# A graph network on one core: one block in place of five ahead of the edge sort, and the zero fill asked for by two engines

## The reference, cut to what matters

```python
q_i = (x @ Wq).reshape(-1, 8, 8)[dst]
k_j = (x @ Wk).reshape(-1, 8, 8)[src]
w   = mlp(edge_attr_8) + mlp(edge_attr_16)        # silu(a @ W1 + b1) @ W2 + b2
alpha = (q_i * w * k_j).sum(-1) / sqrt(8) * edge_weight
out = segment_sum(alpha[..., None] * (x @ Wv)[src].reshape(-1, 8, 8), dst) / 32
x = layernorm(x + out)
# then three more layers over the same edges: 3 smoothing steps with a threshold,
# 5 powers of the normalised adjacency, 2 graph convolutions
```

## Time and profile before

| what | us |
|---|---|
| median of three runs | 8149.56 |
| the profiled execution | 8145.88 |
| its span, first to last instruction | 8144.0 |
| zero fill asked for (ACT's 100 requests) | 2.46 to 234.85 |
| first request of the sort | 414.76 |
| first scatter of the sort | 447.10 |
| last scatter of the sort | 2911.28 |
| PE busy over the span | 6943.6 (85%) |
| DVE / ACT / POOL busy | 5918.6 / 4418.0 / 2861.5 |

### The profile page before, as it was taken

The page is one execution under the profiler, slowest core; times in us unless marked ns, Lnnn a source line. Parts: engine busy times, 40 slices in busy tenths (PEclk is TensorE's granted clock), DMA queues, the critical chain, the costliest instruction groups (busy, mean ns, idle before and its releaser), DMA issues. The chain is left out here.

```text
span 8144.0 us, 280276 instructions
## 1 busy us (share of the span) xinstructions
PE 6943.6 (85%) x98699; PEld 5906.3 (73%) x98724; DVE 5918.6 (73%) x17405; ACT 4418.0 (54%) x13288; POOL 2861.5 (35%) x2957
## 2 busy tenths in 40 slices
PE   0289999999999989999996588788896899998887
PEld 0155555555555579999996588788896888897877
DVE  1266666666666679899896799799899666676556
ACT  0222222222222269999996587687796565665545
POOL 0068888888888855455454000000000000000000
PEclk9999999999999999999998799999998999998889
DMA  9222232222322247767665688787895666664545
GB/s 383 113 55 61 59 61 59 60 59 60 60 60 61 59 157 231 230 227 230 226 228 174 231 300 292 276 298 283 291 332 205 201 197 197 197 192 137 171 134 157
DMA packets 656410, 1425.57 MB, mean 175 GB/s; under 512 B 284336, under 2 KB 351662, under 8 KB 652737
## 3 DMA queue, kind: packets, MB, share of 16 engines
q1 hardware_dynamic: 538370, 1220.03, 46.6%
q0 software_dynamic: 101792, 92.82, 5.5%
q10 hardware_dynamic: 15700, 105.61, 3.2%
HBM read 982.95 MB, written 433.34 MB: 174 GB/s over the span
## 5 line engine op out<-in xcount | busy, mean ns | idle before, releaser
L243 POOL DMA_INDIRECT sorted_rows<-sort_rows,sort_row_at x1600 | 1975.2, 1234 | 518.0 <-issue 496.4
L1560 ACT ACTIVATE smooth_msg<-smooth_ps_a,smooth_w_rows 128x64 f32<-128x64 f32 x6000 | 1311.6, 333 | 313.3 <-PE smooth_ps_a L1646 297.1
L273 ACT ACTIVATE sort_count<-sort_ps_c 50x50 bf16<-50x50 f32 x1600 | 331.9, 207 | 1983.8 <-PE sort_ps_c L305 1348.2
L1341 ACT ACTIVATE poly_cast<-poly_mat 128x1536 bf16<-128x1536 uint8 x500 | 714.2, 1475 | 462.3 <-PE poly_ps L1362 362.8
L301 PEld LDWEIGHTS sort_ps_r<-sort_count,sort_hot_dt 50*125 50x125 bf16 x1600 | 283.3, 177 | 836.5 <-issue 639.1
L315 PE MATMUL sort_ps_m<-sort_w,sort_hidden 128*125 128x64 f32 x3200 | 879.3, 430 | 0.0
L1668 PE MATMUL smooth_ps_s<-smooth_msg,smooth_hot 128*128 128x64 bf16 x7500 | 769.1, 194 | 76.8 <-DVE smooth_last_part L1799 67.0
L294 PE MATMUL sort_ps_h<-sort_attrs,sort_w 24*128 24x500 f32 x800 | 812.6, 1117 | 2.5 <-DMA sort_attrs<-in_attr_t 2.5
L1668 PE MATMUL smooth_ps_s<-smooth_last_part,smooth_hot 128*128 128x64 bf16 x7500 | 763.6, 194 | 15.9 <-issue 15.9
L1668 PE MATMUL smooth_ps_s<-smooth_rest,smooth_hot 128*128 128x64 bf16 x7500 | 764.7, 194 | 14.3 <-issue 14.3
L1668 PEld LDWEIGHTS smooth_ps_s<-smooth_msg,smooth_hot 128*128 128x128 bf16 x7500 | 685.8, 99 | 111.9 <-DVE smooth_last_part L1799 68.9
(11 more groups left out here) (332 smaller groups left out, 16487.0 us busy)
## 6 DMA issues: line engine op xcount, KB each, us to landing
poly_mat<-counts_t SPq DMA_DIRECT2D x500, 400.0 KB
smooth_src<-src_rows SPq DMA_DIRECT2D x150, 960.0 KB, 5.0
smooth_hot<-hot_rows SPq DMA_DIRECT2D x150, 960.0 KB, 6.9
smooth_src<-src_rows SPq DMA_DIRECT2D x150, 640.0 KB, 6.0
smooth_hot<-hot_rows SPq DMA_DIRECT2D x150, 640.0 KB, 6.3
sorted_rows<-zeros ACTq DMA_DIRECT2D x100, 875.0 KB, 13.3
graph_edges<-sorted_rows SPq DMA_DIRECT2D x125, 700.0 KB
hot_rows<-graph_hot SPq DMA_DIRECT2D x125, 640.0 KB, 3.4
```

What stands on the lines that cost most here:

```text
L243: pool.indirect_dma_start(out=sorted_rows, out_offset=bass.IndirectOffsetOnAxis(row_at[u][:, j:j + 1], 0), in_=rows[u][:, j, :], in_offset ...
L1341: act.activation(cast[u][h][:, DVE_S:HR, :], mat[u][h][:, DVE_S:HR, :], ACT.Copy)\
L1560: last = act.activation(at[:, i, :], ps_a[g % 2][:, i * D:(i + 1) * D], ACT.Copy, scale=w_rows[u][:, c * CHUNK + i:c * CHUNK + i + 1])
```

## The change

The blocks `prepare`, `load_tables`, `project` (its first use alone; the convolutions still call it) and `split_qkv` become one block, `front`. SP asks for x, the weights and the two tables right behind the three column loads. PE transposes straight from x, four node blocks into one PSUM bank; DVE copies each four transposes at once (64 x 500) and each two products at once (125 x 384). ACT computes nothing in it. The scratch tiles of the edge tables lie in `q_parts` and `kv_parts`, so the split of q waits until the keys and blocks have landed, and it writes its remainders to `node_sums` (not in use yet) in place of `qkv`, so it needn't wait for the store of `qkv`. ACT asks for 72 of the 100 transfers of zeros in this block, SP for 28 in the sort, behind the loads of groups 0 and 1.

```diff
+ZERO_DMAS = 2 * NB
+ZERO_EARLY = 72
+def fill_zeros(eng, sorted_rows, zeros, zeroed, begin, end):
+    view = sorted_rows[0:N_SLOTS, :].rearrange("(k b) c -> k (b c)", b=NB // 2)
+    for b in range(begin, end):
+        eng.dma_start(view[b * CAP:(b + 1) * CAP, :], zeros[:]).then_inc(zeroed, 16)
 ...
+        under_kv = kv_parts[:].rearrange("p b i d -> p (b i d)").bitcast(F32)
+        under_q = q_parts[:].rearrange("p b i d -> p (b i d)").bitcast(F32)
+        ends = under_kv[:, 0:2 * NT].bitcast(I32).rearrange("p (e t) -> p e t", e=2)
+        node, lane, block_d, block_s = (under_kv[:, i * NT:(i + 1) * NT] for i in range(2, 6))
+        rest = node_sums[:].rearrange("p b c -> p (b c)")[:, 0:NB * D]
 ...
             @blk.scalar
             def _(act):
                 act.wait_ge(zeros_made, 1)
-                for b in range(2 * NB):
-                    act.dma_start(view[b * CAP:(b + 1) * CAP, :], zeros[:]).then_inc(zeroed, 16)
+                fill_zeros(act, sorted_rows, zeros, zeroed, 0, ZERO_EARLY)
 ...
             @blk.sync
+                sp.dma_start(x[:], ...).then_inc(tables_in, 16)     # Wq, Wk, Wv, ident, iota too
                 sp.wait_ge(cols_read, 2)
                 sp.dma_start(ends[:, 0, :], io["dst"]...).then_inc(rows_in, 16)
                 sp.dma_start(ends[:, 1, :], io["src"]...).then_inc(rows_in, 16)
+                sp.wait_ge(kept, NB // 2)
+                sp.dma_start(qkv_rows..., qkv...).then_inc(rows_out, 16)
                 sp.wait_ge(rows_ready, 1)
 ...
-                sp.wait_ge(rows_out, 32)
+                sp.wait_ge(rows_out, 48)
+            @blk.tensor
+                def products(i):
+                    b, e = groups[i]
+                    pe.wait_ge(turned_sb, i + 1)
+                    for j in range(b, e):
+                        if j % 2 == 0 and j >= 4:
+                            pe.wait_ge(kept, j // 2 - 1)
+                        last = nc.tensor.matmul(ps_o[j // 2 % 2][0:NL, (j % 2) * 256:(j % 2) * 256 + 3 * D],
+                                                xt[i % 2][:, (j - b) * NL:(j - b + 1) * NL], w_qkv[:], ...)
+                        if j % 2 == 1:
+                            last.then_inc(product, 1)
+                pe.wait_ge(tables_in, 96)
+                for i, (b, e) in enumerate(groups):
+                    if i >= 2:
+                        pe.wait_ge(turned_sb, i - 1)
+                    for j in range(b, e):
+                        last = nc.tensor.transpose(ps_t[i % 2][...], x[:, j, :], ident[0:NL, 0:NL])
+                    last.then_inc(turned, 1)
+                    if i >= 1:
+                        products(i - 1)
+                products(len(groups) - 1)
             @blk.vector
+                def keep(i):
 ...
+                def parts(to, whole):
+                    left = rest.rearrange("p (b d) -> p b d", d=whole.shape[2])
+                    link(dve.tensor_copy(to[:, :, 0, :], whole))
+                    link(dve.tensor_tensor(left, whole, to[:, :, 0, :], ALU.subtract))
+                    link(dve.tensor_copy(to[:, :, 1, :], left))
+                    link(dve.tensor_tensor(to[:, :, 2, :], left, to[:, :, 1, :], ALU.subtract))
 ...
+                dve.wait_ge(tables_in, 96)
+                for i in range(len(groups) + 1):
+                    keep(i)
                 dve.wait_ge(rows_in, 32)
 ...
+                dve.wait_ge(kept, NB // 2)
+                for h in two:
+                    at = slice(h * half, (h + 1) * half)
+                    parts(kv_parts[:, at], qkv[:, at, D:3 * D])
+                dve.wait_ge(rows_out, 48)
+                parts(q_parts, qkv[:, :, 0:D])
@@ sort_edges
                 for u in two:
                     loads(u, slice(u * G * TE, (u + 1) * G * TE))
+                fill_zeros(sp, sorted_rows, zeros, zeroed, ZERO_EARLY, ZERO_DMAS)
 ...
-                pool.wait_ge(zeroed, 32 * NB)
+                pool.wait_ge(zeroed, 16 * ZERO_DMAS)
```

More of the change, by code:

```diff
@@ L63, in prepare @@
[L63 to L68, removed]
+        two = range(2)
+        under_kv = kv_parts[:].rearrange("p b i d -> p (b i d)").bitcast(F32)
+        under_q = q_parts[:].rearrange("p b i d -> p (b i d)").bitcast(F32)
@@ L71, in prepare @@
+        groups = [(b, min(b + QUAD, NB)) for b in range(0, NB, QUAD)]
         with nc.Block() as blk:
@@ L105, in link, with places @@
                     dve.wait_ge(step, n[0])
-                def split(which, block, read):
-                    link(dve.tensor_copy(node[:], ends[:, which, :]))
+                def places(which, block, read):
+                    link(dve.tensor_copy(node, ends[:, which, :]))
                     if read:
                         dve.sem_inc(cols_read, 1)
[L112 to L115, removed]
@@ L126, in _ @@
[L126 to L133 removed]
+                    link(dve.tensor_scalar(lane, node, 1.0 / NB, -0.49, ALU.mult, ALU.add))
@@ new lines, in places @@
+                    link(dve.tensor_scalar(lane, lane, 12582912.0, None, ALU.add))
+                    link(dve.tensor_scalar(lane, lane, 12582912.0, None, ALU.subtract))
+                    link(dve.scalar_tensor_tensor(block, lane, -float(NB), node, ALU.mult, ALU.add))
+                def keep(i):
+                    if i < len(groups):
+                        b, e = groups[i]
+                        dve.wait_ge(turned, i + 1)
+                        if i >= 2:
+                            dve.wait_ge(product, groups[i - 2][1] // 2)
+                        dve.tensor_copy(xt[i % 2][:, 0:(e - b) * NL], ps_t[i % 2][0:D, 0:(e - b) * NL]).then_inc(turned_sb, 1)
+                    if i >= 1:
+                        b, e = groups[i - 1]
+                        for j in range(b, e, 2):
+                            dve.wait_ge(product, j // 2 + 1)
+                            dve.tensor_copy(qkv[:, j:j + 2, :], ps_o[j // 2 % 2][0:NL, :]
+                                            .rearrange("p (a c) -> p a c", a=2)[:, :, 0:3 * D]).then_inc(kept, 1)
@@ L479, in _ @@
                                         ps_o[u][0:NL, 0:n_out]).then_inc(kept, 1)
[L482 to L532, removed]
-                split(kv_parts, qkv[:, :, D:3 * D])
 N_RP = NB // 2
@@ L2023, in build @@
                 tbl = sb("tbl", [NL, NT, 8], F32, sorting)
-                prepare(nc, io, tbl, key_rows, block_rows, sorted_rows, zeros, zeroed)
                 with ExitStack() as projecting:
```

69 lines of the change are left out of this document (49 added, 20 removed).

## The result

The changed kernel took 8033.19 us in the median of 4 runs (8026.84 to 8040.06), against 8150.18 before: 117 us less, a ratio of 0.9858 with a 95% interval of 0.9845 to 0.9870. Forecast was 8012 with a range of 7998 to 8030, a gain of 137. So the direction and most of the size came, 20 us did not, and the time lies 3 us outside the range. Later sets of the same kernel had medians of 8039.54 and 8030.79, 114 and 127 us under the runs of before beside them; so the gain is 114 to 127, and 137 in none of the three. The profiled execution was the slowest of its set, 8040.06 with a span of 8038.4.

The account below looks back on a forecast made before the run. Front bound in two independent halves, DMA (zero fill paced by five engines) and dependent compute; the loop's start sets the end. First scatter 136 us earlier, PE's loop 138, so 137 off: 8009 profiled, 8012 median, range 7998 to 8030.

Parts of the forecast that it names:

- steps 3 and 4: Sort's start: constants and first groups' loads 8 us, SP's 28 transfers of zeros 61 us; fill and first scatter at 311.
- the sum: Whole kernel: 8145.9 - 137 = 8009 for the profiled execution, 8012 for the median; each group's 12.31 us stay.
- step 5: Start of the sort's loop: DVE may once wait for POOL's group 0, 0 to 2 us, counted in the 137.
- Step 1: Merged front: five engines move 31.4 MB at 130 GB/s, done at 244 us; ACT's last request about 230.
- the test on that kernel: Five-engine arithmetic on the kernel before: 2.5 + (28.0 + 4.8 + 1.6) / 0.131 = 265, against 266.2 for x and tables.
- Step 2: SP's chain in the front: tables 68, store asked for at 128, keys 143, stores landed 213 to 215, q 226 us.
- the step's other figure, 175: Store of q, k and v in the front: done near 175 us if DMA engines take packets in turn.
- The cover: End of the front: q done at 226 us against 230 for ACT's requests, so SP's chain is hidden by 4 us.
- The rival of the slower loop: Sort's loop locks onto POOL's pace: 0.69 us more a group cancels the gain; 8170 or 8864 us possible; chance 0.03.

Follow-up runs that it names:

- experiment 1: Changed kernel with all 100 transfers of zeros asked for by ACT in the front, none by SP in the sort: 8037.71 us, ratio 0.9859 to the kernel before.
- experiment 2: Changed kernel with 56 transfers of zeros asked for by ACT in the front and 44 by SP in the sort: 8026.35 us, ratio 0.9847.
- experiment 3: Changed kernel with each 125-row transfer of the front asked for as 112 rows and 13: 7982.94 us, ratio 0.9792 to the kernel before.
- experiment 4: Kernel before with its five blocks, but 28 transfers of zeros asked for by SP in the sort: 8138.43 us, ratio 0.9987.
- experiment 6: Changed kernel with the sort's ten constant loads asked for in the front, behind the row loads: 8026.77 us, ratio 0.9845 to the kernel before.
- experiment 9: Padding: kernel before with 96 PE products 8152.05, with 40 DVE operations 8152.51; changed kernel with the products 8014.69, then 8022.79; split-rows, early-constants, 50-early kernel with them 7982.87.

## Why the prediction was wrong, point by point

**What failed, in short.** Two things. The time at which the zero fill lands and lets the first scatter go (steps 3 and 4) was put at 311 us and measured at 320.6. And the stages behind the sort stood in the sum at nothing, without a reason; in three profiles they took 7 to 18 us more than in the one of before. The restart of the loop (step 5) cost 4.4 us, not 0 to 2, in one profile of three.

**The reading of the bound was right.** Two halves that need nothing from each other; the end moves with the last thing that starts the loop; in the changed kernel that thing is the zero fill; the fill goes at the pace of five engines. Experiments 1 to 4 and 6 put other inputs into the same arithmetic. Their first scatters came in or at the edge of what it gave: 336.3 for 330 to 340, 321.8 for 318 to 322, 272.9 for 255 to 275, 432.0 for 432 to 436, 318.8 for 314 to 320. Those forecasts were made with the changed kernel's profile in hand. The landings were later than computed in 1 (309.3 for 304) and in 3 (271.6 for 247).

**Step 1 (72 transfers and SP's work, 244 us) held, to 4 us.** ACT's last request, made at 223.4, ended at 225.2 (230 forecast) and landed 25 us later, at 248.4. The "about 250" that the step has for the kernel before is too early as well: the request of 233.0 landed 35.7 us later, at 268.7. So the test on that kernel, 265 against the 266.2 of the tables, is 3.7 us short of the fill itself; taken to that, the five engines' pace is 129 GB/s and not 131.

**Step 2 (SP's chain) had the order right and nearly each size too long.** Tables at 63.8 (68); PE takes 3.82 us for four blocks, 0.96 each, not 1.14, so the store is asked for at 112 (128); keys at 127.1 (143); store and keys landed at 180.5 (213), 68 us for 5.6 MB, better than half share and nearer to the step's other figure, 175; q done at 191.3 (226). The cover was 34 us, not 4. It decided nothing.

**Steps 3 and 4 (constants 8, fill 61, scatter at 311) are the steps that failed.** From 250.6, where SP begins to ask for its zeros, to the last landing at 319.3 it took 68.7 us; the step had 61, from 252 to 313. POOL's scatter followed 1.3 us later. So 6.3 us are the landing, 2 the choice of 311 where the sum gave 313, and 1.3 the way from landing to scatter: 9.6. Where the 6.3 lie: the step's bytes for the five engines come to 31.4 + 1.06 + 7.84 = 40.3 MB, and they landed in 316.8 us, so the mean pace was 127 GB/s and not 130. The profile shows slower stretches at the start (278 GB/s on all 16 in the first 10 us) and at 245 to 250 (97 GB/s at a share of 0.31); how much each cost wasn't separated. The constants and the loads of groups 0 and 1 took SP 24 us of asking, not 10: a request for a constant took 1.2 to 5.9 us while ACT's transfers were queued. So the step's sentence that the DMA engines don't stop was wrong for eleven of them. It looked like the culprit and isn't: asking for the constants early gained 1.8 us (experiment 6).

**Step 5 (restart, 0 to 2 us) was too low in one profile.** The loop took 4.4 us more there than before, with DVE's waits, and no more than before in two others. The rival of the slower loop named the mechanism, a loop held to POOL's pace, and was far off in size: its smallest price was 0.69 us a group, and 4.4 us are 0.02.

**What the sum had no term for: the stages behind the sort.** Against the one profile of before, with a gain of 137 us forecast (us):

| profile of the changed kernel | first scatter | sort | behind the sort | short of 137 |
|---|---|---|---|---|
| first | 10.5 | +4.8 | +16.1 | 31.4 |
| second | 10.6 | +0.3 | +18.1 | 28.9 |
| third | 10.3 | -0.8 | +6.9 | 16.3 |

The medians of the three sets are 20, 23 and 10 us short, less than the profiles: the one of before, 8145.88, was a fast execution (the sets of before have medians of 8150.18, 8153.46 and 8157.82), and the first of the changed kernel lies 7 us over its median. So about 10 us of what is missing are shown as the late fill, and the rest lies behind the sort, most of it in smoothing. Part of it may be the spread from one execution to the next, and its cause is open (experiment 9). The range was drawn from the front alone; it should have had room for a program of 8 ms whose untouched stages differ by 5 us in the mean between builds, and by 11 us between profiles of one and the same kernel.

The Trainium skill ("DMA: Bandwidth & Descriptors", section "Why a DMA increments its semaphore by 16 and not by 1") gives a transfer the largest number of engines up to 16 that divides its slowest dimension: 16 for 112 rows, 5 for 125. The trace agrees in both: a share of 0.31 where 125-row transfers run alone, and 50 us less in experiment 3. The Trainium skill also says that asking from another engine saves only the time of asking ("DMA: Bandwidth & Descriptors", section "Issuing engines are not separate DMA queues"). Experiments 1 and 2 agree: with 56 or 72 transfers asked for by ACT the first scatter is at 321.8 and 320.6, and with all 100 it comes later only because the front ends later.

## What to carry to other kernels

Look for stretches in which the DMA share stands at a simple fraction: 0.31 is five engines of 16, and the count of rows says why. Such a bound hardly moved here with who asked and when, as long as the five engines stayed busy (56 or 72 transfers, constants early or late: first scatters from 318.8 to 321.8 us); it moved with the shape of the transfers. Splitting each 125-row transfer in 112 + 13 rows gave nearly half as much again as the whole change. Test such arithmetic on the landing that it is to forecast, not on one near it. And in a long program give the range a term for the stages that aren't touched.

## What the runs showed that was not expected

- The 125-row transfers from SP got more than half of the five engines beside the fill in one case: q, k, v, keys and blocks, 5.6 MB in 68 us, 82 GB/s of some 130, against 68 GB/s for the columns. Rows of 38 KB against 6.4 KB may be the reason; it wasn't tried.
- An SP request of a small constant took 1.2 to 5.9 us while ACT's transfers were queued (up to 15.0 in experiment 6), and 0.3 to 0.6 in the kernel before, where no zeros were under way: there the same ten requests took 5 us, here 19.
- The sort's loop has two modes in one and the same program: DVE never waits for a scatter, or waits in most groups. The pace is 12.30 to 12.31 us a group without the waits and 12.30 to 12.36 with them.
- Smoothing differs by 10 us in the mean between builds in which it is the same code, and the graph stage by 5 the other way. Open.
